# A transformer tower on one core: low parts of x on VectorE, first passes over the FFN weights on GpSimd in quarters, last products in the wide banks

## The reference

```python
h = _L0_tok_ref(x, L0_tok_W, ...)                    # patches @ W.T + b, class token, + pos_enc
h = h + _L0_attn_ref(_layernorm(h), ...)             # z = sigmoid(..), c = .., h_t = (1-z_t) h + z_t c_t
h = h + _L0_ffn_ref(_layernorm(h), W_fc, ..., W_proj)
h = h + _L1_attn_ref(_layernorm(h), ...)             # rotary, causal softmax attention over 37 tokens
h = h + _L1_ffn_ref(_layernorm(h), ...)              # round to 8 bits, ternary weight, bias

def _absmean_core(W):                                # on W_fc (1024x256) and on W_proj (256x1024)
    gamma = jnp.mean(jnp.abs(W)) + EPS
    Ws = W / gamma
    return jnp.sign(Ws) * jnp.minimum(jnp.round(jnp.abs(Ws)), 1.0)
```

## Time and profile before

| | |
|---|---|
| runs, us | 157.62, 156.41, 157.09; median 157.09 |
| profiled execution | 157.96 us, of which the span from the first to the last instruction is 155.9 us |
| mean granted TensorE clock | 0.977 of full speed |
| busy: PE, DVE, ACT, POOL | 146.1, 129.8, 104.0, 87.6 us |

### The profile page before, as it was taken

The page is one execution under the profiler, slowest core; times in us unless marked ns, Lnnn a source line. Parts: engine busy times, 40 slices in busy tenths (PEclk is TensorE's granted clock), DMA queues, the critical chain, the costliest instruction groups (busy, mean ns, idle before and its releaser), DMA issues.

```text
span 155.9 us, 3371 instructions
## 1 busy us (share of the span) xinstructions
PE 146.1 (94%) x1003; PEld 128.1 (82%) x1003; DVE 129.8 (83%) x395; ACT 104.0 (67%) x254; POOL 87.6 (56%) x139
## 2 busy tenths in 40 slices
...
GB/s 167 310 404 400 415 395 240 3 4 115 22 0 0 4 0 90 225 2 6 0 2 2 8 2 0 4 4 2 2 2 0 6 0 0 6 31 58 58 117 49
DMA packets 5728, 12.31 MB, mean 79 GB/s; under 512 B 1120, under 2 KB 3024, under 8 KB 5328
## 3 DMA queue, kind: packets, MB, share of 16 engines
...
## 4 chain that ended last, share of the span: by engine, by line
PE 59%; DVE 18%; issue 6%; POOL 6%; DMA 4%; SPq 3%; ACT 1%; DVEq 0%; POOLq 0%
PE bank L481 36%; PE bank L635 5%; POOL x_lo L1338 5%; DMA x_raw<-x_in 4%; SPq L424 3%; PE bank L714 3%; PE bank L575 3%; PE bank L699 3%; DVE stats L970 3%; DVE hs L1153 2%; POOL small L1314 2%; DVE residual L1289 2%; PE bank L559 2%; DVE zc L1143 2%; DVE hs L1169 2%
## 5 line engine op out<-in xcount | busy, mean ns | idle before, releaser
L1314 POOL TENSOR_TENSOR small<-small,powers 119x1 f32<-119x1 f32 (+3 forms) x51 | 36.8, 724 | 40.4 <-DVE small L982 27.2
L1338 POOL TENSOR_TENSOR x_lo<-x_raw,x_hi 128x714 fp32r<-128x714 f32 x8 | 14.6, 1831 | 11.6 <-ACT x_hi L788 11.6
L481 PE MATMUL bank<-pj,gt_hi 128*119 128x256 f32 x80 | 20.1, 290 | 0.0
L481 PE MATMUL bank<-pj,gt_lo 128*119 128x256 f32 x80 | 19.4, 281 | 0.0
L888 ACT ACTIVATE gt_hi<-bank 128x476 fp32r<-128x476 f32 x20 | 11.1, 570 | 7.1 <-PE bank L635 7.0
L1379 POOL TENSOR_TENSOR qk<-rope 128x476 f32<-128x476 f32 (+1 forms) x12 | 12.2, 1039 | 5.8 <-DVE rope L1241 5.8
L481 PE MATMUL bank<-fc,n1t_hi 128*119 128x512 f16 x40 | 15.2, 379 | 0.0
L481 PE MATMUL bank<-fc,n1t_lo 128*119 128x512 f16 x40 | 15.1, 378 | 0.0
L559 PE MATMUL bank<-wt_hi,x_hi 128*119 128x256 f32 x48 | 13.9, 289 | 1.4 <-ACT x_hi L788 0.8
L481 PEld LDWEIGHTS bank<-pj,gt_lo 128*119 128x119 f32 x80 | 14.5, 181 | 0.0
L481 PEld LDWEIGHTS bank<-pj,gt_hi 128*119 128x119 f32 x80 | 14.4, 181 | 0.0
...
## 6 DMA issues: line engine op xcount, KB each, us to landing
...
```

What stands on the lines that cost most here:

```text
L481: last = mm(out, a, b, start=(n == 0), stop=(n == len(pairs) - 1))
L1314: return gt(small[0:held(i, r), i, r:r + n], small[0:held(i, r), i, mv + 1:mv + 2 * n:2], powers[0:held(i, r), 0:n], ALU.pow)
L1338: gt(x_lo[:, i, :, 0:n], x_raw[:, i, :, 0:n], x_hi[:, i % X_SLOTS, :, 0:n].bitcast(F32), ALU.subtract).then_inc(s["x_lo_ready"], 1)
```

## The change

1. POOL's step split:i is gone. DVE has split:2 to split:9 in its string: the same subtraction.
2. w_below goes from DVE to POOL, and both passes are done in four pieces of 128x512 a matrix: w_below:0 to 3 and w_ternary:0 to 3 for fc, 4 to 7 for pj. fc_ready and pj_ready are waited for at 4 instead of 1.
3. out:i goes from the narrow ring to the wide one. On TensorE its bias product now stands ahead of the wait for q3t.
4. All four strings of ORDER are written anew. Among others w_pos:0 on DVE stands ahead of w_tok:1, and TensorE does seat:0 ahead of tok:1.

The diff, cut to its core:

```diff
 RINGS = {
-    "narrow": ((0, 1), (..., "attend", "out")),
+    "narrow": ((0, 1), (..., "attend")),
     "turned": ((2, 3, 4), ("t0", "t1", "tg", "t2", "turn", "t3")),
-    "wide": ((5, 6, 7), ("gate", "fc", "qk")),
+    "wide": ((5, 6, 7), ("gate", "fc", "qk", "out")),
...
+        def piece(w, q):
+            k = w.shape[1]
+            if k >= PIECES:
+                return slice(k // PIECES * q, k // PIECES * (q + 1)), slice(0, w.shape[2])
+            per, width = PIECES // k, w.shape[2] * k // PIECES
+            return slice(q // per, q // per + 1), slice(q % per * width, (q % per + 1) * width)
...
             def out_(i):                                   # TensorE
                 n = seen_rows(i)
                 out = claim(("out", i))
+                if i == 0:
+                    pe.wait_ge(s["out_rows_ready"], 2)
+                mm(out[0:n, 0:D], pick[0:STACK, 0:n], out_rows[0:STACK, :], start=True, stop=False)
                 pe.wait_ge(s["q3t_ready"], i + 1)
                 if i == 0:
                     pe.wait_ge(s["w_out_ready"], 1)
-                    pe.wait_ge(s["out_rows_ready"], 2)
-                mm(out[0:n, 0:D], pick[0:STACK, 0:n], out_rows[0:STACK, :], start=True, stop=False)
...
-            def w_below(n):                                # DVE
-                out, w, _ = ternary[n]
-                dve.wait_ge(s["cut_ready"], 2)
-                ts(out[:, :, :], w[:, :, :], derived[:, D_NEG_CUT + n:D_NEG_CUT + n + 1], None, ALU.is_lt)\
-                    .then_inc(s["below_ready"], 1)
-            def w_ternary(n):
+            def w_ternary(u):                              # DVE
+                n, q = divmod(u, PIECES)
                 out, w, ready = ternary[n]
-                dve.wait_ge(s["below_ready"], n + 1)
+                ks, cols = piece(w, q)
+                dve.wait_ge(s["below_ready"], u + 1)
...
-            def split(i):                                  # POOL
-                n = ROWS
-                pool.wait_ge(s["x_hi_ready"], i - FULL_TILES + 1)
-                gt(x_lo[:, i, :, 0:n], x_raw[:, i, :, 0:n], x_hi[:, i % X_SLOTS, :, 0:n].bitcast(F32),
-                   ALU.subtract).then_inc(s["x_lo_ready"], 1)
+            def w_below(u):                                # POOL
+                n, q = divmod(u, PIECES)
+                out, w, _ = ternary[n]
+                ks, cols = piece(w, q)
+                pool.wait_ge(s["cut_ready"], 2)
+                nc.gpsimd.tensor_scalar(out[:, ks, cols], w[:, ks, cols], derived[:, D_NEG_CUT + n:D_NEG_CUT + n + 1], None, ALU.is_lt)\
+                    .then_inc(s["below_ready"], 1)
```

More of the change, by code:

```diff
@@ L121 @@
     "tensor": """
-        warm:0 tok:0 tok:1 seat:0 seat:1 tok:2 t0:0 seat:2 tok:3 t0:1 seat:3 w_gate:0 t0:2 tok:4 t0:3 seat:4
-        w_ternary:0 tok:5 t0:4 seat:5 tok:6 tok:7 seat:6 tok:8 seat:7 t0:5 seat:8 tok:9 w_fold:0 seat:9 t0:6
-        w_fold:1 t0:7 t0:8 gate:0 w_value_bias:0 gate:1 gate:2 gate:3 w_ln_bias:0 gate:4 gate:5 h1:0 h1:1 t0:9
-        gate:6 h1:2 h1:3 gate:7 t1:0 gate:8 t1:1 gate:9 gate:10 fc:0 t1:2 fc:1 gate:11 h1:4 h1:5 fc:2 fc:3 t1:3
-        h1:6 fc:4 h1:7 tg:0 tg:1 fc:5 fc:6 fc:7 t1:4 tg:2 tg:3 proj:0 fc:8 tg:4 t1:5 fc:9 tg:5 proj:1 fc:10 h1:8
@@ new lines @@
+        tok:5 t0:2 seat:5 tok:6 tok:7 t0:3 t0:4 seat:6 seat:7 tok:8 seat:8 t0:5 tok:9 w_fold:0 seat:9 t0:6
+        w_fold:1 t0:7 gate:0 w_value_bias:0 t0:8 gate:1 gate:2 gate:3 gate:4 w_ln_bias:0 gate:5 t0:9 h1:0 h1:1
+        gate:6 h1:2 gate:7 h1:3 t1:0 gate:8 gate:9 gate:10 t1:1 fc:0 fc:1 t1:2 gate:11 h1:4 h1:5 fc:2 h1:6 h1:7
+        fc:3 t1:3 fc:4 tg:0 fc:5 tg:1 fc:6 t1:4 fc:7 tg:2 proj:0 tg:3 fc:8 tg:4 fc:9 tg:5 t1:5 proj:1 fc:10
+        fc:11 t1:6 tg:6 h1:8 tg:7 proj:2 h1:9 fc:12 tg:8 t1:7 fc:13 tg:9 proj:3 tg:10 t2:0 fc:14 proj:4 t1:8
@@ new lines @@
+    "vector": """
+        w_ones:0 w_tok:0 w_pos:0 w_tok:1 w_pos:1 stats0:0 split:2 w_gamma:0 split:3 stats0:1 mean0:0 mean0:1
+        n0:0 w_small:0 split:4 stats0:2 stats0:3 mean0:2 n0:1 w_gate:0 mean0:3 stats0:4 mean0:4 w_gate_bias:0
+        split:5 t0:0 w_cut:0 split:6 t0:1 n0:2 n0:3 stats0:5 n0:4 mean0:5 split:7 w_ternary:0 split:8
+        w_ternary:1 split:9 w_ternary:2 stats0:6 mean0:6 stats0:7 n0:5 t0:2 t0:3 stats0:8 mean0:7 mean0:8 t0:4
+        n0:6 t0:5 n0:7 stats0:9 mean0:9 w_fold:0 n0:8 t0:6 n0:9 t0:7 w_fold:1 w_ternary:3 w_ternary:4
+        w_ternary:5 w_qk:0 w_ternary:6 w_ternary:7 gate:0 t0:8 gate:1 scan:0 scan:1 w_ln_bias:0 scan_left:0
+        w_value_bias:0 h1:0 h1:1 stats1:0 mean1:0 stats1:1 h1:2 mean1:1 t0:9 stats1:2 gate:2 h1:3 mean1:2 gate:3
+        stats1:3 t1:0 scan:2 scan:3 gate:4 scan_left:1 mean1:3 t1:1 gate:5 h1:4 h1:5 fc:0 stats1:4 t1:2 gw:0
+        mean1:4 stats1:5 t1:3 square:0 h1:6 fc:1 tg:0 gw:1 tg:1 scan:4 mean1:5 t1:4 fc:2 stats1:6 gw:2 scan:5
+        square:1 mean1:6 tg:2 h1:7 tg:3 proj:0 stats1:7 tg:4 stats2:0 t1:5 fc:3 mean1:7 gw:3 scan_left:2 tg:5
+        proj:1 fc:4 gw:4 t1:6 h1:8 square:2 mean2:0 stats2:1 stats1:8 tg:6 tg:7 proj:2 fc:5 h1:9 mean1:8 tg:8
+        gw:5 square:3 t1:7 tg:9 mean2:1 fc:6 stats1:9 square:4 stats2:2 mean2:2 mean1:9 proj:3 tg:10 t2:0
+        stats2:3 proj:4 stats2:4 square:5 tg:11 square:6 gw:6 mean2:3 t1:8 mean2:4 t2:1 t2:2 proj:5 t2:3 fc:7
+        tg:12 gw:7 stats2:5 square:7 mean2:5 fc:8 tg:13 gw:8 rope:0 proj:6 stats2:6 tg:14 t1:9 square:8 tg:15
+        mean2:6 rope:1 tg:16 proj:7 stats2:7 t2:4 mean2:7 tg:17 score:0 sbias:0 fc:9 score:1 sbias:1 gw:9 t2:5
+        t2:6 proj:8 score:2 sinv:0 t2:7 sbias:2 stats2:8 mean2:8 score:3 tg:18 square:9 tg:19 rope:2 attend:0
+        sinv:1 proj:9 sinv:2 stats2:9 mean2:9 stats3:0 sbias:3 mean3:0 sinv:3 rope:3 attend:1 t2:8 t2:9 attend:2
+        stats3:1 mean3:1 clip:0 stats3:2 attend:3 score:4 round:0 sbias:4 mean3:2 rope:4 score:5 sbias:5
+        stats3:3 score:6 mean3:3 sinv:4 clip:1 rope:5 attend:4 sinv:5 sbias:6 score:7 stats3:4 sbias:7 attend:5
+        clip:2 stats3:5 round:1 mean3:4 round:2 score:8 mean3:5 sinv:6 sinv:7 score:9 sbias:8 clip:3 sbias:9
+        attend:6 sinv:8 out:0 stats3:6 attend:7 clip:4 mean3:6 round:3 round:4 out:1 sinv:9 stats3:7 score:10
+        attend:8 mean3:7 clip:5 sbias:10 stats3:8 out:2 attend:9 mean3:8 clip:6 round:5 round:6 sinv:10 out:3
+        stats3:9 out:4 mean3:9 clip:7 attend:10 out:5 stats3:10 round:7 clip:8 mean3:10 round:8 out:6 clip:9
+        out:7 round:9 out:8 clip:10 round:10 out:9 out:10""",
```

110 lines of the change are left out of this document (42 added, 68 removed).

## The result

The changed kernel takes **159.33 us** (159.18 to 161.62, 4 runs), the kernel before in the same session 157.01 (156.41 to 157.62, 4 runs). The ratio is 1.0144, with a 95% interval of 1.009 to 1.0198: **2.3 us slower**. In a second session it was 160.07 against 157.00, 1.0182 (1.0137 to 1.0227). The forecast was 156.8, a little faster. Its range (154.4 to 159.9) holds the time, its sign is wrong. The ratios leave out executions more than 1.5 per cent above the kernel's fastest, such as the 161.62 us here, one of 208.22 us of d1 and one of 495.61 us of g1.

A forecast was written before the change was run, and what follows sets the result against it. POOL and DVE were taken to bound the kernel up to 60 us, then TensorE for some 75 us. Start +0.6 and end -0.9 made -0.3 on 157.96: 157.66, or 156.8 on the median's scale; range 154.4 to 159.9.

The forecast's parts named there:

- up to the cut: From the kernel's start to the end of w_cut (L1085): claimed to stay at 23.85 us, no change.
- from the cut to n0:9 (the walk): DVE and POOL steps followed in order behind w_cut: DVE's n0:9 waits for POOL's h0:9 until 40.3 us; before, 40.47.
- from n0:9 to scan:1's end: DVE's last stretch of the start: 9.3 us instead of 8.55, for one quarter more and four instruction starts.
- order of the rest: The new order of the 75 us in which TensorE is the bound: counted as zero, since its work is the same.
- the end: Last tiles out:8 to out:10: bias product during the q3t wait saves 0.3 us each, 0.9 together; third bank gains nothing.
- price P of a piece: Time of one 128x512 piece of w_below on POOL: taken as 1.13 us.
- my three bounds: Estimates for a w_below piece on POOL: 1.13 us from two-input rows, 1.56 from its tensor_scalar, some 0.6 from the CAST.
- six two-input instructions in a row: Three splits and three quarters on DVE until 32.3 us, shutting out POOL's h0:5, which ends at 33.0.
- rival 2: POOL's row becomes the slower bound in the start: pieces from 1.56 us, +2.8 us in all, 159.9 us; chance 0.18.
- its two signs: Mean of L1343 (POOL's pieces) 1.5 us or more, and DVE's n0 waits for POOL's powers above 4 us.
- 60 to 136 us at zero: The stretch where TensorE is the bound: claimed not to change by more than half a microsecond.
- The chance given to slower: Whole kernel: probability 0.21 of a measured time above 158.7 us.

The follow-up runs named there:

- d1: The changed kernel with TensorE's small w_gate products put back ahead of tok:4, where they stood before the change; ratio 1.0170 to the kernel before.
- g1: The changed kernel with the eight w_below pieces on DVE instead of POOL, which keeps the powers; ratio 1.0233 to the kernel before.
- a1: The kernel before with only the change's two edits for the last products (wide banks, bias product ahead of the q3t wait); 156.25 us, ratio 0.9893.
- h1_fold_late: The kernel before with TensorE's w_gate products moved behind tok:4; 161.38 us, ratio 1.0289.
- a4: The changed kernel with w_out_bias on POOL moved behind proj:8, far from the start; ratio 1.0054 to the kernel before.
- r1_after: The changed kernel run once more, nothing altered, in the second session; 160.07 us, ratio 1.0182 to the kernel before.
- a3: The changed kernel with each of POOL's eight w_below pieces cut to one column instead of 512; ratio 1.0045 to the kernel before.
- f2: The kernel before with only the bias product moved ahead of the q3t wait, still in the narrow banks; ratio 0.9937.

## Why the prediction was wrong

The forecast's terms beside those of the changed kernel's first profile, in which the clock didn't fall in the start (us more than before):

| term | forecast | measured |
|---|---|---|
| up to the cut | 0 | -0.2 |
| from the cut to n0:9 (the walk) | -0.2 | +0.7 |
| from n0:9 to scan:1's end | +0.75 | +1.7 |
| order of the rest | 0 | +0.85 |
| the end | -0.9 | -1.5 |
| sum | -0.3 | +1.5 |

The order of the rest is the changed kernel against a1, the end a1 against before; in all three the clock had fallen by out:10. The measured sum is that of the two spans (155.9 and 157.4). The prediction also took off 0.87 us, by which the profiled execution of before lay above the median. The changed kernel's profiled execution lay at its median (159.18 and 159.33), so this isn't in the +1.5, and with it the 2.3 us of the times are reached. In before's profile the clock fell at 148.8 us, ahead of out:8 to out:10, and h1_fold_late's last step is 1.0 us sooner without that: this is likely what the 0.87 are.

**The start up to the cut** was right within 0.2 us: 23.68 and 24.02, forecast 23.85 unchanged.

**The price P of a piece** was mis-sized: 1.13 forecast, 1.56 measured. Of my three bounds the one from POOL's own tensor_scalar was exact (1.56), and I took a value between it and rows of another kind of instruction because the 0.93 us "may hold something else". It didn't (0.94 in a4, far from the start). The statement of the Trainium skill ("GPSIMD Engine Reference", section 4.1, one-input instructions roughly line-rate on GpSimd) doesn't hold here: 1.56 us against 0.47 to 0.51 on DVE.

**The walk to n0:9** missed by 0.7 us only, 40.97 measured and 40.3 forecast, because two errors nearly cancelled; that is luck. The seven pieces ahead of h0:9 were 0.43 us longer each, 3.0 in all. But POOL was not shut out by six two-input instructions in a row: h0:5 ended at 30.66, held by one split, where I had 33.0, and w_below:3 was the one held next (2.93). In r1_after w_below:3 took 3.74 us, the longest that I saw, beside three instructions in a row. That is why rival 2, whose price was the true one, didn't bring its 43.4 for h0:9 and its +3.7. Of its two signs one came, the mean of L1343 (1.88 us), and one didn't: n0:7 and n0:9 waited 1.3 us for powers together, not above 4. Holding shows in both directions: w_ternary:0 took 1.18 instead of 0.74 beside a piece, pieces of fc took 2.15 (median) and 2.93 instead of 1.56. The splits, though, took 0.85 and 0.89 beside the same pieces, no more than alone. "SBUF — State Buffer" in the Trainium skill, "Who interferes with whom", describes a full block for whoever comes second; POOL's long rows agree. For DVE behind POOL it isn't borne out: the quarter lost 0.44 us beside pieces of 1.56, and no split lost any.

**From n0:9 to scan:1's end** is the step that failed most, by 0.9 us: forecast 9.3, measured 10.23, before 8.55. The 9.3 were right for the work, since with w_out_bias away it was 9.47. What I left out is that w_out_bias now stands behind the late pieces and runs beside five quarters, where before it ran beside a pass and wq_lo and was itself the one held (CAST 3.42, 1.41 now, 0.40 free in a4).

**TensorE's clock** wasn't in the forecast for the start at all: 0.9 us in the executions in which it fell.

So the start lost 2.35 us without the fall and 3.2 with it, where I had 0.6. Taken off r1_after's 3.2 one at a time, the pieces make 1.55 (up to 0.3 of it the later fall of the clock in a3), the held quarters 0.75 and the clock 0.9; such terms needn't add up.

**60 to 136 us at zero** was wrong: "its work is the same" is true, but the new order of it costs 0.85 to 1.15 us in the traces at the same clock, and some 1 per cent in the times. So this step failed by as much as the one before it. Which step of the new order costs it stays open.

**The end** was right in its number for the bias product (1.0 us in the times, 0.9 forecast), and only in part in its mechanism. I had 0.3 us for each of three tiles in one chain; at the same clock the traces show 0.2 to 0.4 in all. The remainder of f2's trace goes with the clock; for the times that isn't shown. The third bank adds 0.4 in the times and 0.6 in the traces, ahead of out:7, which I had put at nothing. In the changed kernel only 0.7 of this shows, because the rest's new order takes 0.85 of a1's 1.5.

With the terms of the traces: start +2.35 to +3.2, order of the rest +0.85, end -1.5; +1.7 to +2.55 against a measured 2.3 (first session) and 3.1 (second). The chance given to slower, 0.21, was too low: the one row of the same instruction spoke for rival 2, and I let the mean of unlike rows outvote it.
